# Which engine copies the turned query features out of PSUM in the second attention's loop

## What is computed

```python
def _softmax_kernel(data, proj, is_query):
    ratio = proj.shape[0] ** (-0.5)
    dn = data.shape[-1] ** (-0.25)
    dash = jnp.einsum('bhnd,md->bhnm', data * dn, proj)
    diag = 0.5 * dn ** 2 * jnp.sum(data * data, axis=-1, keepdims=True)
    if is_query:
        stab = jnp.max(dash, axis=-1, keepdims=True)
    else:
        stab = jnp.max(dash, axis=(-2, -1), keepdims=True)
    return ratio * (jnp.exp(dash - diag - stab) + EPS)
...
qp = _softmax_kernel(q, proj, True)
kp = _softmax_kernel(k, proj, False)
k_sum = jnp.sum(kp, axis=2)
d_inv = 1.0 / jnp.einsum('bhnm,bhm->bhn', qp, k_sum)
context = jnp.einsum('bhnm,bhnd->bhmd', kp, v)
out = jnp.einsum('bhnm,bhmd,bhn->bhnd', qp, context, d_inv)
```

## Time and profile before

| | |
|---|---|
| median of 3 runs | 1765.59 us (1764.76 to 1766.38) |
| the profiled execution, its span | 1762.0 us |
| of it the loop, turns 7 to 79 | some 172 us |
| TensorE busy over the span | 1715.6 us, 97% |
| VectorE, ScalarE, GpSimd busy | 743.4, 396.1, 653.0 us |

### The profile page before, as it was taken

One profiled execution on the slowest core, in us unless ns is written; L12 is line 12 of the kernel. 1 busy time (PEld: TensorE's weight loads), 2 busy tenths in 40 slices (PEclk: granted clock), 3 DMA queues, 4 the chain that ended last, 5 costly groups with the idle time before them and its releaser, 6 DMA issues. The chain is left out here.

```text
span 1762.0 us, 21030 instructions
## 1 busy us (share of the span) xinstructions
PE 1715.6 (97%) x8016; PEld 1068.0 (61%) x8016; DVE 743.4 (42%) x1549; ACT 396.1 (22%) x740; POOL 653.0 (37%) x537
## 2 busy tenths in 40 slices
PE   9999999998999999999999999898999999999998
PEld 6466445544444677755477775555776676677633
DVE  5886011322732432154455553854333322222237
ACT  1100000001411000111177771841100222222232
POOL 0666884031000047767787862000210312222213
PEclk9999999998999999999999999999999999999999
DMA  9654116074170034333322223705262899999951
GB/s 352 200 168 123 2 1 167 1 214 120 73 297 5 0 96 127 98 96 101 92 49 57 53 48 79 195 11 195 60 198 87 351 415 415 400 415 411 412 150 59
DMA packets 103755, 281.71 MB, mean 160 GB/s; under 512 B 61745, under 2 KB 69155, under 8 KB 91282
## 3 DMA queue, kind: packets, MB, share of 16 engines
q1 hardware_dynamic: 28755, 218.54, 33.4%
q0 software_dynamic: 67872, 50.79, 12.8%
q10 hardware_dynamic: 7052, 11.35, 1.9%
HBM read 250.37 MB, written 29.80 MB: 159 GB/s over the span
## 5 line engine op out<-in xcount | busy, mean ns | idle before, releaser
L608 POOL DMA_INDIRECT table_d<-wring x85 | 173.9, 2046 | 106.3 <-issue 66.7
L380 PE MATMUL bank<-wring,region_a 128*125 128x512 f32 x480 | 207.6, 593 | 1.7 <-DVE region_a L754 0.7
L993 POOL DMA_INDIRECT wring<-xl_d,wring x85 | 111.2, 1308 | 255.2 <-DMA xr_d<-flat_b 229.3
L380 PEld LDWEIGHTS bank<-wring,region_a 128*125 128x125 f32 x480 | 89.7, 188 | 115.3 <-issue 113.9
L1006 POOL DMA_INDIRECT score_d<-wring x85 | 108.8, 1280 | 72.1 <-DMA score_d<-wring 42.7
L396 PE MATMUL bank<-flat_d,wring 128*128 128x312 f32 (+1 forms) x512 | 135.0, 426 | 0.0
L2403 PEld LDWEIGHTS bank<-picked_t,wring 128*128 128x128 f32 x1152 | 129.4, 192 | 7.7 <-issue 7.7
L2403 PE MATMUL bank<-picked_t,wring 128*128 128x128 f32 x1152 | 131.3, 276 | 0.0
L993 POOL DMA_INDIRECT wring<-xr_d,wring x85 | 110.4, 1299 | 25.9 <-issue 24.7
L396 PEld LDWEIGHTS bank<-flat_d,wring 128*128 128x128 f32 x512 | 96.8, 189 | 37.8
L2410 PE MATMUL bank<-wring,small_t 128*64 128x256 f32 x640 | 76.0, 393 | 2.8 <-PEq L2037 2.8
(11 more groups left out here) (441 smaller groups left out, 2671.6 us busy)
## 6 DMA issues: line engine op xcount, KB each, us to landing
wring<-in_experts SPq DMA_DIRECT2D x57, 2048.0 KB, 19.5
wring<-in_L_Ws SPq DMA_DIRECT2D x6, 2048.0 KB, 15.8
table_d<-eq_buf SPq DMA_DIRECT2D x2, 3072.0 KB, 26.9
score_d<-no_edge SPq DMA_DIRECT2D x2, 3072.0 KB, 32.1
wring<-table_d POOLq DMA_DIRECT2D x10, 610.4 KB, 7.1
wring<-score_d SPq DMA_DIRECT2D x5, 1093.8 KB
wring<-pid_d ACTq DMA_DIRECT2D x17, 312.5 KB, 3.8
wring<-in_edge_w ACTq DMA_DIRECT2D x17, 312.5 KB, 4.4
```

What stands on the lines that cost most here:

```text
L380: ins = pe.matmul(bank[0:R, :], act_t[:, k, tok(t)], w[:, k * HALF:(k + 1) * HALF], start=(k == 0), stop=(k == chunks - 1))
L608: pool.indirect_dma_start(out=tables_d[b % 2], out_offset=bass.IndirectOffsetOnAxis(ap=edge_at[:, b:b + 1], axis=0), in_=edge_sums[:, b, : ...
L993: pool.indirect_dma_start(out=to[:, g % 2, j, :], out_offset=None, in_=table, in_offset=bass.IndirectOffsetOnAxis(ap=index[:, b:b + 1], ax ...
```

## The change

The copy L1827 leaves ScalarE's list and a `tensor_scalar` with the same factor and addend enters VectorE's. It waits for the same two semaphores and raises the same one. In VectorE's turn it stands behind L1678, L1680 and the head's output (L1687, L1689), and ahead of the context copies and the edge step. TensorE's list is untouched. In the changed file the lines below the insertion are numbered 8 higher up to the place of the removal.

```diff
@@ -1689,6 +1689,14 @@
                         v.tensor_tensor(o1[:, :, h * DH:(h + 1) * DH], rows_o[:, :, 0:DH],
                                         row_den[:].unsqueeze(2).to_broadcast([R, T, DH]), ALU.mult)\
                             .then_inc(hsem["o_copied"], 1)
+                    q = u - Q_LAG - 2
+                    if 0 <= q < UNITS:
+                        v.wait_ge(hsem["q_turned"], q + 1)
+                        if q >= 2:
+                            v.wait_ge(hsem["q_used"], q - 1)
+                        turned = banks[3][0:MC, 0:3 * R].rearrange("p (c r) -> p c r", r=R)
+                        v.tensor_scalar(qf_t[:, q % 2, :, :], turned, RATIO, EPS_F * RATIO, ALU.mult, ALU.add)\
+                            .then_inc(hsem["q_feat"], 1)
                     k = u - 2
                     if 0 <= k < UNITS and k % T == T - 1:
                         h = k // T
@@ -1818,14 +1826,6 @@
                             s.wait_ge(hsem["k_used"], u - 1)
                         s.activation(kf[:, u % 2, :], banks[0][0:R, 0:M], ACT.Exp, bias=neg_k[:, t, h:h + 1])\
                             .then_inc(hsem["k_exp"], 1)
-                    q = u - Q_LAG - 2
-                    if 0 <= q < UNITS:
-                        s.wait_ge(hsem["q_turned"], q + 1)
-                        if q >= 2:
-                            s.wait_ge(hsem["q_used"], q - 1)
-                        turned = banks[3][0:MC, 0:3 * R].rearrange("p (c r) -> p c r", r=R)
-                        s.activation(qf_t[:, q % 2, :, :], turned, ACT.Identity, scale=RATIO,
-                                     bias=eps_ratio[0:MC, 0:1]).then_inc(hsem["q_feat"], 1)
                     if u < UNITS:
                         s.wait_ge(hsem["k_exp"], u + 1)
                         s.activation(kf[:, u % 2, :], kf[:, u % 2, :], ACT.Identity, scale=RATIO,
```

## The result

The changed kernel takes 1805.59 us (median of 4 runs, 1803.13 to 1805.83); the kernel before, beside it, 1765.20 us. The ratio is 1.0205, with a 95% interval of 1.0178 to 1.0232: 40.4 us slower. I had predicted 1799.8 us, 34.6 us slower, in a range of 1790 to 1814.

What follows compares the result with a forecast made beforehand. TensorE was taken as bound by its own work. Losses of 32.7 us to turn 80 and 4.3 at the loop's end, less 2.8 back, net 34.2: span 1796.2, plus 3.6 for the median, 1799.8 us; range 1790 to 1814.

Steps and rivals of the forecast that it cites:

- The place and its margin: In the loop, the transposes wait for the copy, which ended only 0.04 us before it would hold TensorE.
- Ordinary turns: 60 loop turns without a head's output, each 0.16 us longer with the copy behind L1678 and L1680: 9.6 us.
- Output turns: 14 loop turns where the copy stands behind L1687 and L1689, waiting for the output product: 1.60 us each, 22.4 us.
- Edge steps: VectorE's steps behind the copy: late ones hidden by 0.1 us, six groups' first steps 0.12 us late each, 0.7 us.
- The rival that VectorE becomes the bound in those turns: 28 turns with an edge step cost 0.1 to 0.2 us more each, giving 1803 to 1806 us; chance 0.13.
- The end of the loop: Turns 81 to 83 take 2.9 us more, and three copies among the last edge steps add 1.4 us.
- The clock: Rival: TensorE's clock falls in the new output-turn gaps, up to 25 us, 1812 to 1824; over 15 us has chance 0.07.
- What comes back: Behind the loop, one scatter out of the way gives back 2.8 us of the 37.0; softmax waits shrink some 3 us.
- signs of being wrong: Output turns staying near 2.5 us, lower clock stretches in the loop, or the turn with a step being the long one.

Runs made afterwards that it cites:

- e3_scalar_later: Kernel before, with the copy kept on ScalarE but one place later in its list, behind L1831; ratio 1.0195 to the kernel before.
- e1_copy_first: Changed kernel with the copy on VectorE moved to the head of its turn, ahead of L1678; ratio 1.0004 to the kernel before.
- e2: Changed kernel with VectorE's copy behind L1680 but ahead of the head's output (L1687, L1689); ratio 1.0110 to the kernel before.
- e4: Kernel before, with VectorE doing the copy only in turns 7, 12, 17, ..., 82 and ScalarE in all others; ratio 1.0140 to the kernel before.
- e12: Changed kernel with the counts of the first two tiles fetched behind the scores of their tile; ratio 1.0200 to the kernel before.

## Why the prediction was right, and where it was off

**The place and its margin: right.** That the copy ended only 0.04 us ahead of holding TensorE was read from two rows, and it carries everything: e3_scalar_later moves the copy by one place without changing its engine and costs 35 us in the loop, and e1_copy_first changes the engine and costs nothing.

**Ordinary turns: right, slightly too large.** 0.127 us a turn instead of 0.16; up to turn 79 they make 7.5 us, where the sum had 9.6 for one turn more. The copy starts at +1.35, ends at +1.90 and is followed by the transposes' load at +2.01, all as worked out. The term that was too large is the last one: from that load to the next turn I had taken 0.52 us from the earlier trace rows, where the load is not held and takes 0.37 us; here it takes 0.34 us and the next turn starts 0.48 us after it (979.17, 979.65). The copy took 0.542 us on average, where I had 0.55 from the two neighbouring shapes.

**Output turns: right.** 3.92 us instead of 3.97, by the same 0.04 us, and 21.8 us instead of 22.4. e2 and e4 show the term by itself, from both sides.

**Edge steps: right.** Hidden but for six turns behind a first step, 0.15 us each (0.12 predicted). The rival that VectorE becomes the bound in those turns did not come true.

**The end of the loop: right in kind, mis-sized.** For turns 81 to 83 I had 2.9 us more; they took 4.1 more (9.6 instead of 5.5). One part is a misreading. I took 5.84 us for them before, from L1678 to L1678, but by the weight loads of the kernel before it is 5.49 us, as the second L1678 was held by the edge step of turn 83:

```profile
1058.87 0.29 PEld L1325 LDWEIGHTS bank<-proj,region_a 64*125 64x125 f32 x2
...
1064.36 0.29 PEld L1325 LDWEIGHTS bank<-proj,region_a 64*125 64x125 f32 x2
```

The other part is the clock: TensorE ran at 1.2 GHz for 10.2 us from turn 82 on, which I had priced only as a rival. From turn 84 to the last scores it was 1.3 us more, where I had 1.4.

**The clock: a term left out of the sum.** I gave up to 25 us to a rival with a chance of 0.07 and nothing to the sum. It was in between: two of 14 gaps, 3.0 us in the loop, and the tail. It belonged in the sum with a few us. The profile after was to show a clock of 1.00 in the loop, and stretches at the lower level were one of my own signs of being wrong: on this point I was. (The rival's 15 to 25 us on 1799.8 would have been 1815 to 1825, not 1812 to 1824.)

**What comes back: the step that failed.** I booked 2.8 us for one scatter out of the way. It was out of the way, but the counts' fetch, which starts with the last scores, met the first two of the last group (7.8 and 5.9 us) where before it had met the one that is now gone (7.7 us). The chain of scatters gave back 1.2 us and TensorE's second wait ended 1.0 us sooner behind the last scores; the waits, which were to shrink by 3 us, stayed at 4.8 us. The earlier trace rows had shown the stalled scatter (7.7 us from 1071.67 to 1079.38); I had counted the scatters and not asked which one would run beside the fetch. e12 supports this in part.

The terms add up: the last scores were 41.0 us later where I had 37.0, 1.0 us came back where I had 2.8, and 1.5 us were added in the rest of the kernel: 41.0 - 1.0 + 1.5 = 41.5 us, where I had 34.2. In part the sum was lucky. The ordinary and output turns were 2.6 us too large, and that hid most of the 3.0 us that the clock cost in the loop; the 1.2 us ahead of turn 7 were in no term. What put the time into the range all the same is that the range was made for a few lost clock levels.

The Trainium skill's figures, page "VectorE: DVE Perf Modes", TRN2 errata, gave an estimate of 0.52 us for VectorE's copy and 0.46 us for ScalarE's. Measured are 0.542 and 0.559 us. So by the page's figures ScalarE would be the faster at this shape, and here VectorE is, by 3%.

## What to carry to other kernels

Where an engine works through an ordered list, ask of a moved instruction not whether the new engine has time, but what stands ahead of it there and what that waits for. An instruction whose inputs come from the turn before belongs at the head of the turn, ahead of those that wait for the present one: on VectorE that place was worth 40 us and the engine nothing that could be measured. And before moving anything on the second-busiest path, measure the margin by which it is hidden: here the profile showed it, 0.15 us against the 0.11 us of a held case.

## What the runs showed of the hardware

In the loop of the changed kernel a gap of TensorE of some 1.5 us between dense turns was followed by 3.4 us at 1.2 GHz in two of 14 cases, in e4_only_output_turns in one of 14, and by nothing in the others; each such stretch cost 1.5 to 1.6 us. The loss is not in proportion to the idle time: in e3_scalar_later every turn is 0.48 us longer, 35 us in all, and its clock is 1.00 from 886 to 1100 us. In the changed kernel and in e12_after_counts_later, whose loops are alike, the same two turns were slow, 43 and 73. That suggests that such a loss goes with the timing of the program; with one profiled execution of each it is not shown, and what picks the gap stays open.

Page "TensorE: Matmul & The Clock Gate" of the Trainium skill, section "What's actually happening", says that the default state is throttled and that activity releases it. The rows agree so far as each fall in a loop came behind a gap of TensorE. They do not say why most gaps were followed by none.

A scatter behind the loop was issued 2.8 to 3.2 us after the one ahead of it in most cases, and 5.9 to 7.8 us after it where the fetch of the counts had just been issued (1111.54 in the changed kernel). With that fetch moved away the last scatter came 2.9 us sooner behind the last scores.
